# A state-space scan kernel: where the backward pass begins its side steps, and which states are forced by a diagonal product

## The reference, cut to what matters

```python
A = -jnp.exp(A_log)
def step(hst, ins):
    dt_t, B_t, C_t, x_t = ins
    dA = jnp.exp(dt_t[:, :, None] * A)
    hst = hst * dA + (dt_t * x_t)[:, :, None] * B_t[:, None, :]
    y_t = jnp.einsum('bds,bs->bd', hst, C_t)
    return (hst, y_t)
...
h_fwd = _ssm(h, fwd_in_w, ...)
h_bwd = jnp.flip(_ssm(jnp.flip(h, 1), bwd_in_w, ...), 1)
x = x + gate * (h_fwd + h_bwd)
```

## Time and profile before

| | |
|---|---|
| median of 3 runs | 3309.45 us (3305.4 to 3314.07) |
| the profiled execution | 3316.36 us, its span 3314.5 us |
| busy share of the span | PE 92%, DVE 87%, ACT 88%, POOL 88% |
| granted TensorE clock, mean | 0.970 |
| HBM traffic | 48 GB/s over the span |

### The profile page before, as it was taken

One profiled execution on the slowest core, in us unless ns is written; L12 is line 12 of the kernel. 1 busy time (PEld: TensorE's weight loads), 2 busy tenths in 40 slices (PEclk: granted clock), 3 DMA queues, 4 the chain that ended last, 5 costly groups with the idle time before them and its releaser, 6 DMA issues.

```text
span 3314.5 us, 71769 instructions
## 1 busy us (share of the span) xinstructions
PE 3058.3 (92%) x23032; PEld 2760.6 (83%) x23032; DVE 2884.0 (87%) x3203; ACT 2904.8 (88%) x6357; POOL 2911.3 (88%) x1552
## 2 busy tenths in 40 slices
PE   8778999999999999999999999999999999998877
PEld 6568988898888988889888898888888898887766
DVE  2269999899989998899998999899988999989985
ACT  1189999898989989899998999899898989989993
POOL 0069999998999999999998999999999999999995
PEclk6699999999999999999999999999999999999998
DMA  5011111111111111111111111112111111111210
GB/s 179 0 42 45 45 46 54 43 52 44 46 51 45 52 44 47 51 50 44 46 54 44 51 45 45 53 45 52 44 47 50 51 46 45 45 50 44 55 47 26
DMA packets 163039, 162.61 MB, mean 49 GB/s; under 512 B 17610, under 2 KB 156874, under 8 KB 162644
## 3 DMA queue, kind: packets, MB, share of 16 engines
q1 hardware_dynamic: 162644, 157.69, 17.5%
HBM read 154.44 MB, written 3.18 MB: 48 GB/s over the span
## 4 chain that ended last, share of the span: by engine, by line
PE 50%; ACT 23%; issue 11%; DVE 8%; POOL 7%; DVEq 0%; ACTq 0%; POOLq 0%; DMA 0%; SPq 0%
PE ps L1263 13%; ACT dA L584 12%; PE ps L1247 12%; ACT uBT L570 6%; PE ps L1010 6%; POOL hst L417 5%; DVE hst L909 5%; PE ps L1245 4%; PE ps L1082 3%; PE ps L1019 3%; PE ps L1057 3%; PE ps L1066 1%; PE ps L1255 1%; PE ps L1131 1%; POOL uBT L430 1%
## 5 line engine op out<-in xcount | busy, mean ns | idle before, releaser
L417 POOL TENSOR_TENSOR hst<-hst,C_sb 128x1024 f32<-128x1024 f32 x1024 | 2447.3, 2407 | 176.1 <-DVE hst L909 172.7
L909 DVE TENSOR_TENSOR_SCAN hst<-dA,ps 128x512 f32<-128x512 f32 x2048 | 2376.7, 1203 | 146.3 <-PE ps L1263 112.9
L584 ACT ACTIVATE dA<-dt,A 128x255 f32<-128x255 f32 x4096 | 1745.0, 501 | 1.4 <-DVE hst L909 1.2
L1263 PE MATMUL ps<-ident,hst 128*128 128x128 f32 x8192 | 1240.7, 274 | 46.8 <-POOL hst L417 46.7
L1247 PE MATMUL ps<-ident,uBT 128*128 128x128 f32 x7104 | 1084.5, 275 | 52.6 <-DVE hst L909 39.8
L570 ACT ACTIVATE uBT<-uT,BT 128x512 f32<-128x512 f32 x1376 | 936.4, 717 | 117.3 <-PE ps L1247 89.2
L1263 PEld LDWEIGHTS ps<-ident,hst 128*128 128x128 f32 x8192 | 963.2, 141 | 62.9 <-POOL hst L417 62.2
L1247 PEld LDWEIGHTS ps<-ident,uBT 128*128 128x128 f32 x7104 | 844.6, 142 | 195.3 <-DVE hst L909 69.4
L430 POOL TENSOR_TENSOR uBT<-uT,BT 128x512 f32<-128x512 f32 x400 | 427.2, 1068 | 1.4 <-PE ps L1245 1.4
L1245 PE MATMUL ps<-uBT,uT 128*128 128x128 f32 x2176 | 302.7, 284 | 33.9 <-DVE hst L909 27.9
L1245 PEld LDWEIGHTS ps<-uBT,uT 128*128 128x128 f32 x2176 | 272.9, 197 | 45.7 <-DVE hst L909 35.9
(11 more groups left out here) (146 smaller groups left out, 2176.0 us busy)
## 6 DMA issues: line engine op xcount, KB each, us to landing
C_sb<-c_dram SPq DMA_DIRECT2D x1024, 128.0 KB, 2.9
gate_l<-gate_rows_dram SPq DMA_DIRECT2D x16, 256.0 KB, 3.8
x_att<-in_x_dram SPq DMA_DIRECT2D x8, 256.0 KB, 3.6
w<-in_L_cond_W_dram SPq DMA_DIRECT2D x2, 1024.0 KB
out_dram<-x_glu SPq DMA_DIRECT2D x8, 256.0 KB, 3.1
wg<-in_L_cond_mlp_w_dram SPq DMA_DIRECT2D x3, 512.0 KB, 11.0
w_xp<-_L_cond_fwd_xproj_w_dram SPq DMA_DIRECT2D x1, 1280.0 KB, 12.5
w_xp<-_L_cond_bwd_xproj_w_dram SPq DMA_DIRECT2D x1, 1280.0 KB, 14.4
```

The source lines that it names most:

```text
L417: pool.tensor_tensor(h, h, C_sb[:, n % FED:n % FED + 1, :].to_broadcast([P, KI, NB]), ALU.mult).then_inc(hC_ready.sem, 1)
L584: done = act.activation(dA[:, n % NT, c, lo:hi], dt[:, d, c, lo:hi], ACT.Exp, scale=A[:, d, c, n:n + 1])
L909: dve.tensor_tensor_scan(pair(hst[:, n % NR]), pair(dA[:, n % NT]), ps[:, BANK_U + (2 * n + e) % (2 * NU), :][:, way], 0.0, ALU.mult, ALU. ...
L1263: last = pe.matmul(ps[:, BANK_Y + j, c * P:(c + 1) * P], hst[:, n % NR, c, j * P:(j + 1) * P], ident[:, :], start=False, stop=(n == NS - 1 ...
```

## The change

Two edits. The lists of states forced by a diagonal lose 1, 3, 61 and 63 (and the last of them, where they hold them) in both directions, so these states are forced in the ordinary way. And the backward pass with a next sequence begins its side steps at half-state 8 (the fifth state) and not at half-state 2 (the second).

```diff
-    BY_DIAGONAL = ((1, 3, 22, 23, 24, 25, 26, 27, 61, 63), (1, 3, 55, 57, 59, 61, 63))
+    BY_DIAGONAL = ((22, 23, 24, 25, 26, 27), (55, 57, 59))
...
-            start = 2 if d == 1 and has_next else FIRST_HALF + 2 * d
+            start = 8 if d == 1 and has_next else FIRST_HALF + 2 * d
```

## The result

| | before | after |
|---|---|---|
| median of 4 runs | 3307.43 us (3300.94 to 3314.07) | 3336.39 us (3334.36 to 3337.86) |
| ratio, 95% interval | | 1.0086 [1.0067, 1.0105] |
| span of the profiled execution | 3314.5 us | 3334.2 us |
| granted clock, mean | 0.970 | 0.965 |

The account below looks back on a forecast made before the run. Each stage has its own bound: POOL sets the pace in plain stretches, PE and DVE under heads steps. -35.0 - 9.8 + 11.2 + 2.8 + 3.4 - 7.5 = -34.9 us gave median 3275, range 3258 to 3299.

Parts of the forecast that it names:

- Part 1: Turn into a backward pass, 7 times: without heads steps C(0) to C(4) falls from 16.32 to 11.3 us, gain 35.0.
- rival A: Slower: the turn's chain, not heads steps, makes 16 us; C(0) to C(4) stays above about 15; median 3346, chance 0.06.
- the chain: PE and DVE work in the turn, from C(63)'s end through `start_y` to two scans: 8.8 us, hidden behind POOL's 11.32.
- Part 2: Heads steps three states later, 7 times: C(4) to C(16) goes from 35.3 to 34.0 us, gain 9.8 in all.
- Part 3: Other 85 steps over 90 half-states, not 96, C(12) to C(60): loss 1.6 us per pass, 11.2 over seven; most 3.2.
- Part 4: 64 diagonals removed, 28 us of POOL's time: loss 2.8 at forward ends, 3.4 in last passes and start; backward ends covered.
- rival C: Clock falls to half in the turns, since transposes do not count as busy PE: +45 us, median 3355, chance 0.03.
- Part 5: Turn into a forward pass behind the jump, 5 times: transposes save PE work, gain 1.5 us each, 7.5 in all.
- B: PE becomes the bound under the denser steps: loss 3.2 us per pass, no heads-step gain; median 3296, chance 0.12.
- the three warnings at the end of the prediction: Wrong if pass 5's first stretch stays above 14, MLP stretches give back over 3 us per pass, or turn's clock falls.

## Why the prediction was wrong, by its steps

**Part 1, the turn: mechanism right, room mis-sized.** The heads steps did make the 16 us: with the start alone the stretch is 11.46 in all seven turns, against 11.32 forecast, and rival A's 15 is excluded. With the diagonals gone too it is 12.30, because the chain is not hidden "with 2.5 us to spare". The chain began at C(63)'s end and took DVE to be free there, as in pass 15, which the part leaned on: its `start_y`, in the kernel before, begins 3.5 us behind C(0) (3099.13), that of pass 5 after the change 5.9 us behind it.

```profile
3102.60 2.05 PE L1255 MATMUL ps<-skip_diag,xsT 128*128 128x128 f32 x16 [0.90 <-DVE gT L895]
```

DVE in order of time after the change, pass 5:

```profile
1158.95 10.11 DVE L909 TENSOR_TENSOR_SCAN hst<-dA,ps 128x512 f32<-128x512 f32 x9
1168.97 1.20 DVE L895 TENSOR_TENSOR gT<-ps,sz 128x1024 f32<-128x1024 f32 x1
...
1174.23 2.33 DVE L909 TENSOR_TENSOR_SCAN hst<-dA,ps 128x512 f32<-128x512 f32 x2 [2.93 <-PE ps L1263]
```

Nine scans stand back to back, none of them waiting, and `gate_y` behind them starts 4.6 us after C(63)'s end (1164.38) where the chain had 1.3 for PE and 1.2 for a scan, 2.5. DVE came out of the forward pass behind, which takes 2.1 of the 2.5 us to spare, and `start_y` at half the clock takes the rest and more.

**Part 2, the heads steps: sign wrong.** "They now enter this stretch 2.5 us ahead of POOL" fails with the same number: there is no lead. POOL idles at once (C(4) of pass 5 waited 0.88 us), and the stretches are 12.77 and 12.19 in place of 12.19 and 11.81, PE busy for all of both. The start alone has the same two, so it is not the clock. C(12) to C(16) is 11.3 before and after: of the 1.4 us of gain per pass nothing came.

**Part 3, the denser steps: the term that decides, outside its bounds.** Forecast 1.6 per pass with 3.2 as the most; measured 6.4. The bound priced the lost half-states in PE's time, and PE was not what ended last in the places that cost most. In C(52) to C(60) it was DVE, with two instructions that had come to stand behind a POOL product (2.4 us per pass, and 15 to 18 us in the time when undone). In C(20), 2.9 us per pass, it was the order of a projection and a norm, shown for 1.2 of them. C(48) alone, 1.2, is of the kind that the forecast meant; C(32), 1.1, stays open. A shift of steps among half-states has no bound in an engine's room, and the first two half-states of it already cost 6 us per pass.

**Part 4 and rival C, the diagonals.** POOL's 1.76 us landed in full at the backward ends with the diagonals alone (C(56) 11.44 to 12.31, C(60) 10.45 to 11.29); after the change DVE sets the pace in C(56) and only the 0.84 of C(60) shows. The forward ends took 0.33 (0.4 forecast), passes 14 and 15 together 0.8 (2.64), pass 0 2.8 (0.72). The cover was there with the old start (1.0001). What the part missed is that the removed diagonals also gained in the old backward turn, and with the new start not: there the turn is at POOL's pace without it, and PE, done earlier, idles 2.68 us, so that the clock falls in six of seven turns. "The trace speaks against it" went from 100 us of plain states at clock 1.00 to turns where PE idles. It holds of the transposes: 40 us of nothing else kept 1.00. The Trainium skill's rule on transposes ("TensorE: Matmul & The Clock Gate", Part 4) would have the clock low there too; these traces don't agree with it, and the falls in the turns go with the idle time, whether real products stand ahead of it or not. The price, 5 us over the seven turns, is far below rival C's 80 us.

**Part 5, the jump.** A gain of 1.5 per turn was forecast and 2.0 came. That the two lie close is luck: the start alone, with its diagonals kept, has 0.8 of it (15.14), and the gain between kernels that differ in the diagonals alone lies between 0.1 and 2.7.

**The rivals.** B named the right place, but priced it at 3.2 per pass, PE's room. Two of the three warnings at the end of the prediction, over 3 us per pass given back and a clock that falls in a turn, came true.

## What to carry to other kernels

When steps are spread over a schedule by a formula, moving its start moves every step's phase against the other engines: price the single long instructions by what they will meet (a two-input SBUF instruction of DVE that starts just behind one of POOL waits it out), not by the engine's average room, and after such a change sweep start and end together. Slack found in a turn must be followed on each engine from where it comes: here DVE was late before the turn began. And work removed ahead of a wait lengthens PE's idle time in it, which can cost the clock.

## What the runs showed of the hardware

- DVE's two-input instruction and POOL's exclude each other for whole instructions: 1.19 us became 2.93 behind a C product, and POOL's 0.62 became 1.64 behind DVE. Half a state of shift for three steps per pass was worth 15 us.
- DVE's instructions with one input in PSUM ran beside POOL unhindered: L740 took 0.69 us in all 680 cases.
- At `start_y` the granted clock went from the 2.4 to the 1.2 GHz level in none of 152 turns with under 1.3 us of idle PE ahead of it, and in 50 of 70 with over 2 us, in kernels that are otherwise alike and in turns with the same rows (`start_y` 3.48 and 2.05 us). With 16 or more real products ahead it fell as often as with none: 18 of 27 and 7 of 10 at 2.0 to 2.5 us.
- Float32 128x128 transposes alone, PE busy 71%, kept clock 1.00 for 40 us.
